# A gated attention and expert block: values in TensorE's waits, heads times values in two parts, and experts in turn by group with three places read early

## The reference, cut to what matters

```python
q = _qdq(x) @ _qdq(wq).T + bq
kv = cond @ wkv.T + bkv                      # k, v
attn = softmax(einsum('bnhd,bmhd->bhnm', q, k) * scale)
o = einsum('bhnm,bmhd->bnhd', attn, v)
x = x + tanh(g0) * (_qdq(o) @ _qdq(wp).T + bp)
...
scores = softmax(h @ gate_weight.T)          # 64 experts in 8 groups of 8
group_scores = scores.reshape(T, 8, 8).max(-1)
_, gidx = top_k(group_scores, 3)             # a token keeps 3 groups
topk_w, topk_i = top_k(where(smask, scores, 0), 6)
slot = flat * 96 + minimum(pos, 95)          # 96 places in each expert
out = (silu(buf @ Wg.T) * (buf @ Wu.T)) @ Wd.T
y = sum(out[slot] * topk_w)                  # six rows of each token
x = x + tanh(g1) * (y + shared(h))
```

## Time and profile before

| | |
|---|---|
| runs | 334.02, 332.68, 329.45 us; median 332.68 |
| profiled execution | 336.5 us, its span 334.6 us |
| granted TensorE clock, mean | 0.974 |
| busy share | PE 86%, DVE 52%, POOL 46%, ACT 33% |
| by stage (us from the span's start) | first loads and units 0 to 41; attention rounds 41 to 87; second norm, shared expert, routing and sort 87 to 131; experts 131 to 307; sums and stores 307 to 334.6 |

### The profile page before, as it was taken

The page is one execution under the profiler, slowest core; times in us unless marked ns, Lnnn a source line. Parts: engine busy times, 40 slices in busy tenths (PEclk is TensorE's granted clock), DMA queues, the critical chain, the costliest instruction groups (busy, mean ns, idle before and its releaser), DMA issues.

```text
span 334.6 us, 5615 instructions
## 1 busy us (share of the span) xinstructions
PE 289.3 (86%) x1963; PEld 178.2 (53%) x1964; DVE 173.8 (52%) x520; ACT 112.0 (33%) x276; POOL 153.8 (46%) x184
## 2 busy tenths in 40 slices
PE   0989858898898989688998799888988898999796
PEld 0455647666653556354554455545544454556674
DVE  2598538895897974342445333543433233333470
ACT  0593144667463343112222112211233233343101
POOL 8415101456605316725766566556655574335000
PEclk9999999999999999979999989999999999999769
DMA  6999940000495002337887788779877882116873
GB/s 220 362 352 379 408 167 2 3 5 2 167 357 192 0 2 63 110 112 257 284 297 245 261 275 297 276 243 317 261 266 249 308 284 100 49 48 198 317 317 125
DMA packets 28880, 68.40 MB, mean 204 GB/s; under 512 B 4374, under 2 KB 11702, under 8 KB 28214
## 3 DMA queue, kind: packets, MB, share of 16 engines
q1 hardware_dynamic: 21840, 54.41, 47.4%
q0 software_dynamic: 5376, 12.59, 10.9%
q10 hardware_dynamic: 1638, 1.05, 1.0%
HBM read 53.09 MB, written 14.94 MB: 203 GB/s over the span
## 4 chain that ended last, share of the span: by engine, by line
PE 71%; DVE 10%; issue 6%; another core or an unknown queue 5%; ACT 4%; DMA 3%; POOL 1%; SPq 0%; DVEq 0%; POOLq 0%
PE psum L1379 22%; PE psum L1396 7%; PE psum L1073 5%; PE psum L1399 5%; PE psum L1435 4%; PE psum L1370 4%; PE psum L1125 3%; PE psum L1268 3%; PE psum L1387 3%; DVE scratch L974 3%; PE psum L1138 2%; DVE order L973 2%; PE psum L1079 2%; PE psum L1440 2%
## 5 line engine op out<-in xcount | busy, mean ns | idle before, releaser
L1379 PE MATMUL psum<-stream,xn 128*96 128x352 f32 x256 | 90.1, 475 | 3.1 <-issue 2.1
L467 POOL DMA_INDIRECT parts<-ctxT,sidx x64 | 59.6, 932 | 62.0 <-ACT ctxT L646 48.4
L1009 DVE COPY rows<-psum 128x192 f32<-128x192 f32 x64 | 22.9, 357 | 86.5 <-PE psum L1388 39.6
L463 POOL DMA_INDIRECT scratch<-table,fetch x48 | 47.1, 982 | 19.7 <-issue 12.5
L1379 PEld LDWEIGHTS psum<-stream,xn 128*96 128x96 f32 x256 | 37.4, 164 | 33.1 <-issue 15.4
L639 ACT ACTIVATE rows<-psum 96x176 f32<-96x176 f32 x43 | 13.5, 314 | 67.4 <-PE psum L1379 36.6
L646 ACT ACTIVATE ctxT<-psum 96x256 f32<-96x256 f32 x64 | 20.8, 375 | 40.3 <-PE psum L1399 21.6
L1396 PE MATMUL psum<-stream,rows 128*96 128x256 f32 x128 | 33.8, 387 | 0.0
L1001 DVE COPY xn<-psum 128x256 f32<-128x256 f32 x48 | 20.1, 418 | 19.7 <-PE psum L1370 14.6
L1387 PE MATMUL psum<-ident,rows 96*128 96x96 f32 x64 | 16.7, 261 | 13.9 <-DVE rows L1009 9.0
L1387 PEld LDWEIGHTS psum<-ident,rows 96*128 96x128 f32 x64 | 9.2, 143 | 30.1 <-issue 24.9
(11 more groups left out here) (215 smaller groups left out, 464.7 us busy)
## 6 DMA issues: line engine op xcount, KB each, us to landing
stream<-wmain_in SPq DMA_DIRECT2D x64, 480.0 KB
parts<-zeros SPq DMA_DIRECT2D x1, 6144.0 KB, 28.4
stream<-parts SPq DMA_DIRECT2D x5, 1024.0 KB, 7.9
stream<-wrem_in SPq DMA_DIRECT2D x32, 112.0 KB
x<-x_in SPq DMA_DIRECT2D x2, 512.0 KB, 6.3
ctxT<-ctxT_in SPq DMA_DIRECT2D x2, 512.0 KB, 7.9
table<-rows SPq DMA_DIRECT2D x8, 128.0 KB, 8.8
parts<-ctxT,sidx POOLq DMA_INDIRECT x64
```

What stands on the lines that cost most here:

```text
L463: g.indirect_dma_start(gx[n % GBUF], None, table, bass.IndirectOffsetOnAxis(fetch[:, j, q:q + 1], 0)).then_inc(got_rows[n % GBUF], 16)
L467: g.indirect_dma_start(parts, bass.IndirectOffsetOnAxis(sidx[:, e:e + 1], 0), orow[e % OBUF], None).then_inc(out_done[e % OBUF], 16)
L1009: v.tensor_copy(hidT[e % 4], bank[6][:, 0:2 * CAP]).then_inc(hidT_done, 1)
L1379: last = t.matmul(bank[UP_BANK[e % (LAG + 1)]][0:CAP, 0:WG], gxT[:, k, CAP * (e % 4):CAP * (e % 4) + CAP], wgu[slot][:, k], start=(k == 0) ...
```

## The change

The program's order changes in four places, beside new banks.

1. Values are made tile by tile (`value_tile`). Tiles 0 and 1 come as before, tile 2 while TensorE waits for the transposed tokens, tiles 3 to 7 in rounds 0 to 2. Units, scores and the projection's weights move up.
2. `heads_times_values` is split from round 3 on: groups 1 and 2 of heads ahead of the scores, 3 and 0 behind the negated maxima. The last two tiles' products stand next to each other, the last in a bank of its own. VectorE's second part of the split maxima (`split_rest`) and the norm of tiles 0 to 3 come later.
3. Experts are worked in turn by group: first the first expert of each group, then the second, and so on; the weights are permuted on the host, and VectorE writes choice and weights in that order. Since a token keeps three groups, at least three of its six experts are worked before the last eight. Places 0, 1 and 2 are read after experts 53, 54 and 55.
4. TensorE sums tiles 0, 1, 4 and VectorE 2, 3, 5, 6, 7; three places are added ahead of the correction on TensorE, four on VectorE.

```diff
...
-PE_TILES, DVE_TILES = (0, 1, 4, 5), (2, 3, 6, 7)
-SUM_BANK = {0: 1, 1: 2, 4: 3, 5: 7}
-CORR_AT = {2: (4, 0), 3: (4, D), 6: (5, 0), 7: (5, D)}
-CORR_STEP = 2
+PE_TILES, DVE_TILES = (0, 1, 4), (2, 3, 5, 6, 7)
+SUM_BANK = {0: 1, 1: 2, 4: 3}
+CORR_AT = {2: (4, 0), 3: (4, D), 5: (5, 0), 6: (5, D), 7: (7, 0)}
+PE_STORES, DVE_STORES = ((0, 2), (4, 1)), ((2, 2), (5, 3))
+EARLY = TOPK - TOPG
+CORR_STEP = EARLY + 1
+
+
+def complete_at(k):
+    return EXPERTS - GROUPS - EARLY + k if k < EARLY else EXPERTS - TOPK + k
+
...
-V_BANK = (5, 4, 6, 7)
-UNIT_BANK = (0, 1, 2, 3, 0, 1, 5, 4)
+V_AT = ((5, 0), (5, D), (4, 0), (7, 0), (6, 0), (6, D), (7, 0), (6, 0))
+V_BEFORE = {0: 6, 1: 8}
+V_SHARED = {0: 2, 4: 6}
+WP_AT = (4, 256)
+UNIT_BANK = (0, 1, 2, 3, 0, 1, 5, 6)
 XQ_BANK = (6, 7, 6, 7)
 ST_BANK = 2
+PV_BANK = (6,) * 7 + (1,)
+PV_SPLIT = 3
 Y_BANK = (7, 7, 7, 7, 2, 3, 2, 3)
...
-        ranked = [cut(TILES * D).rearrange("p (b h) -> p b h", b=TILES) for _ in range(TOPK)]
+        place_rows = lambda: cut(TILES * D).rearrange("p (b h) -> p b h", b=TILES)
+        ranked = [place_rows() for _ in range(1, TOPK - 1)]
+        over = cut(TILES * EXPERTS).rearrange("p (b e) -> p b e", b=TILES)
+        ranked += [place_rows()]
+        cut(2 * (RING * MAINW + PAIRS * D) - TILES * (EXPERTS + (TOPK - 1) * D))
+        ranked = [place_rows()] + ranked
         overT = cut(TILES * P, EXPERTS).rearrange("p (b t) -> p b t", t=P)
-        over = cut(TILES * EXPERTS).rearrange("p (b e) -> p b e", b=TILES)
...
-            first_final = EXPERTS - TOPK
-            for e in range(first_final - OBUF + 1, first_final):
-                sp.wait_ge(out_done[e % OBUF], 16 * (e // OBUF + 1))
+            written = complete_at(0) - OBUF
             for k in range(TOPK):
-                e = first_final + k
-                sp.wait_ge(out_done[e % OBUF], 16 * (e // OBUF + 1))
+                while written < complete_at(k):
+                    written += 1
+                    sp.wait_ge(out_done[written % OBUF], 16 * (written // OBUF + 1))
                 if k < TOPK - 1:
                     sp.dma_start(ranked[k], rank_rows(k)).then_inc(got_ranked[k], 16)
...
             pool.wait_ge(xp_done, TILES)
             for b in range(2, TILES):
+                heads_to_int(b - 2)
                 if b == TILES - 1:
                     norm2_rstd(0)
-                heads_to_int(b - 2)
                 if 3 <= b < TILES - 1:
                     residual(b - 3)
             heads_to_int(TILES - 2)
...
                 if b >= 3:
                     project(b - 3)
             exponential(TILES - 1, 0)
+            exponential(TILES - 1, 1)
             heads_out(TILES - 2)
-            exponential(TILES - 1, 1)
             heads_row(TILES - 4)
+            heads_out(TILES - 1)
             act.wait_ge(nmr_done, 3)
             second_norm(0)
-            heads_out(TILES - 1)
             second_norm(1)
             heads_row(TILES - 3)
             second_norm(2)
...
...
-                v.tensor_scalar(sel[:, n], eout[:, n, 0:EXPERTS], CHOSEN, None, ALU.is_equal).then_inc(sel_done, 1)
+                v.tensor_scalar(in_turn(sel[:, n]), by_group(eout[:, n, 0:EXPERTS]), CHOSEN, None, ALU.is_equal).then_inc(sel_done, 1)
...
                     link(v.scalar_tensor_tensor(out=pexp, in0=eout[:, :, 0:EXPERTS], scalar=CHOSEN, in1=pexp, op0=ALU.is_equal, op1=ALU.mult))
+                    link(v.tensor_copy(in_turn(weight), by_group(pexp)))
                     dve.wait_ge(rankS_done, 1)
                 elif i % 2:
-                    link(v.scalar_tensor_tensor(out=one_rank, in0=rankS, scalar=float((i - 3) // 2), in1=pexp, op0=ALU.is_equal, op1=ALU.mult))
+                    link(v.scalar_tensor_tensor(out=one_rank, in0=rankS, scalar=float((i - 3) // 2), in1=weight, op0=ALU.is_equal, op1=ALU.mult))
...
             def attend(b):
+                if b >= 2:
+                    heads_normalised(b - 2, b % 2)
+                    if b + 1 < TILES:
+                        split_rest(b + 1)
+                    heads_scale(b - 2)
+                    heads_rscale(b - 2)
                 if b == TILES - 1:
                     stats2(b - 4)
                     norm2_veps(0)
-                if b >= 2:
-                    heads_normalised(b - 2, b % 2)
-                    heads_scale(b - 2)
-                    heads_rscale(b - 2)
+                if b == 2:
...
+                if b == 2:
+                    value_tile(7)
                 if b + 2 < TILES:
                     maximum(b + 2, 1)
                 if 4 <= b < TILES - 1:
                     stats2(b - 4)
                 if b + 2 < TILES:
                     maximum(b + 2, 0)
+                    if b == 1:
+                        value_tile(6)
                     split_max(b + 2)
-
...
+                    if b == 0:
+                        split_rest(b + 2)
+
+            maximum(0, 1)
+            maximum(0, 0)
+            split_max(0)
+            split_rest(0)
+            dve.wait_ge(wT_done, 2)
+            value_tile(2)
+            dve.wait_ge(tanh_done, 1)
+            v.tensor_scalar(bvp[:, 1], bvp[:, 1], tg[:, 0:1], None, ALU.mult).then_inc(tbp_done, 1)
+            maximum(1, 1)
             dve.wait_ge(w_psum, 3)
-            v.tensor_scalar(wscale[:], bank[5][:, 256:512], tg[:, 0:1], None, ALU.mult).then_inc(wT_done, 1)
-            for b in range(TILES):
+            v.tensor_scalar(wscale[:], bank[WP_AT[0]][:, WP_AT[1]:WP_AT[1] + 256], tg[:, 0:1], None, ALU.mult).then_inc(wT_done, 1)
+            maximum(1, 0)
+            split_max(1)
+            split_rest(1)
+            value_tile(3)
+            attend(0)
+            value_tile(4)
+            value_tile(5)
+            for b in range(1, TILES):
                 attend(b)
-            norm2_nmr(0)
             heads_normalised(TILES - 2, 0)
             heads_scale(TILES - 2)
             heads_rscale(TILES - 2)
+            norm2_nmr(0)
...
-            def heads_times_values(b):
+            def heads_times_values(b, groups=range(4)):
                 pe.wait_ge(exp_done, 2 * b + 2)
-                pe.wait_ge(headsT_done, b)
-                pe.wait_ge(v_done, b + 1)
-                if b >= 2:
-                    pe.wait_ge(oT_done, min(b - 1, TILES - 4))
-                for g in range(4):
+                pe.wait_ge(v_done, V_BEFORE.get(b, TILES))
+                if PV_BANK[b] == 6:
+                    pe.wait_ge(headsT_done, b)
+                    if b >= 2:
+                        pe.wait_ge(oT_done, min(b - 1, TILES - 4) - (0 not in groups))
+                else:
+                    pe.wait_ge(max_done, 2 * TILES)
+                for g in groups:
                     for i in range(4):
                         h = 4 * g + i
-                        last = t.matmul(bank[6][VW * i:VW * i + VW, TOK * g:TOK * g + TOK], vpad[:, b, h], probs[b % 2][:, TOK * h:TOK * h + TOK],
+                        last = t.matmul(bank[PV_BANK[b]][VW * i:VW * i + VW, TOK * g:TOK * g + TOK], vpad[:, b, h], probs[b % 2][:, TOK * h:TOK * h + TOK],
                                         start=True, stop=True)
-                last.then_inc(pv_psum, 1)
+                if 0 in groups:
+                    last.then_inc(pv_psum, 1)
...
...
                 scores_t(b)
                 if b >= 2:
                     heads_across(b - 2)
+                if b >= PV_SPLIT:
+                    heads_times_values(b - 1, (1, 2))
                 if b >= 3:
                     heads_row(b - 3)
+                if b == 0:
+                    value_tile(3)
+                elif b == 1:
+                    value_tile(5)
+                elif b == 2:
+                    pe.wait_ge(headsT_done, 1)
+                    value_tile(7)
                 if b + 2 < TILES:
                     scores(b + 2)
+                if b == 0:
+                    pe.wait_ge(v_done, 4)
                 negmax_across(b + 1)
-                if b >= 1:
+                if b == 0:
+                    value_tile(4)
+                if b >= PV_SPLIT:
+                    heads_times_values(b - 1, (3, 0))
+                elif b >= 1:
                     heads_times_values(b - 1)
+                if b == 1:
+                    pe.wait_ge(nm_done, 3)
+                    value_tile(6)
                 if b >= 3:
                     pe.wait_ge(nm_done, b + 2)
                     project(b - 3)
...
                 b = TILES - 1
                 scores_t(b)
-                heads_times_values(b - 1)
                 heads_across(b - 2)
                 heads_row(b - 3)
+                heads_times_values(b - 1)
+                heads_times_values(b)
                 pe.wait_ge(norm_done, b - 1)
                 heads_across(b - 1)
-                heads_times_values(b)
                 project(b - 3)
...
             scores(0)
-            xq_across(2)
-            xq_across(3)
             pe.wait_ge(xqT_done, 4)
             pe.wait_ge(v_done, 2)
```

(26 more changed lines are left out.)

84 lines of the change are left out of this document (46 added, 38 removed).

## The result

The change took **321.50 us** (median of 4 runs, 318.97 to 321.75) beside 333.13 for the kernel before (4 runs, 329.45 to 334.02): ratio 0.965 with a 95% interval of 0.957 to 0.974, 11.6 us faster. 319.6 was forecast. The profiled execution took 321.54 (span 319.7, before 334.6). A median here is that of all runs of a kernel, while ratios and their intervals leave out executions in a slower state (over 1.5% above the fastest of their kernel), so that a ratio need not be the quotient of two medians.

What follows compares the result with a forecast made beforehand. It took TensorE's serial work ahead of the loop and late place reads in the tail as bounds; -6.6 + 1.0 + 0 + 1.0 - 8.8 + 0.3 = -13.1 us, taking the median from 332.68 to 319.6 us, range 316 to 323.

Steps and rivals of the forecast that it cites:

- Ahead of the loop: Before the attention loop: moving six values tiles out of TensorE's series starts transposed scores at 34.2 instead of 40.80, -6.6 us.
- Values tiles in the loop: Attention rounds: tile 6 adds 0.65 and tile 7 adds 0.35, the other tiles fit into waits; +1.0 us.
- heads times values in two parts: Attention loop from round 3: half moves ahead of the scores, VectorE's maxima still set the round; 0 us.
- The end of attention: Behind the loop: later norm delays ScalarE's normalised rows, tile 7's product comes earlier; +1.0 us, bounds -0.5 and +2.5.
- rival 1: Tail: TensorE's clock falls all the same, tail gains only 5.3 us, time 323.1; chance 0.14.
- The reads: Expert stage: early reads of places 0 to 2 make no one wait; 0 us.
- The tail: After the experts: early reads and three TensorE tiles keep full clock, end at 325.8; -8.8 us, bounds -9.6 and -5.7.
- The rest: Among the experts: VectorE's copy of weights into the new order and the strided choice cost +0.3 us (0 to 0.8).
- 2 (given back in the loop): Attention: first window overruns in rounds 2 to 5, norm rows cost 2.5; 4.6 us more, 324.2; chance 0.13.
- 3 (reads late): Tail: first data come as late as now, only TensorE's smaller share helps; tail -2, 326.4; chance 0.10.
- 4 (stalls of "another core or an unknown queue"): Expert stage: an earlier start may move these 17 us of waits; doubled, 336.6; chance 0.05.
- range of 316 to 323: Whole kernel: the forecast's own range in us, from bounds of the tail and end of attention, each alone; chance 0.58.

Runs made afterwards that it cites:

- e10: e9 with heads times values in one piece (PV_SPLIT = 8 instead of 3): 322.85 us, ratio 0.967 to the kernel before.
- e5: The changed kernel run again, unaltered, beside other variants: 301.19 us, ratio 0.966 to the kernel before (311.77 there).
- e1: Only the change's attention part; expert order, reads and tile division as in the kernel before: 330.74 us, ratio 0.984 to the kernel before.
- e7: The changed kernel with all six places read after the 59th scatter and later, as before: 309.74 us, ratio 0.989 to the kernel before.
- e8: The changed kernel with tail tiles divided four on TensorE and four on VectorE, as before: 300.07 us, ratio 0.966 to the kernel before.
- e4: The changed kernel with four unused products in TensorE's two waits at the end of attention: 322.55 us, ratio 0.960 to the kernel before.
- e6: The changed kernel with both the norm placement of e3 and the fill products of e4: 298.63 us, ratio 0.958 to the kernel before.
- e9: The kernel of e6 run again in another comparison: 323.17 us, ratio 0.967 to the kernel before (335.57 there).
- e2: The kernel before with only the expert turn, early reads and three/five tile division: 329.16 us, ratio 0.985 to the kernel before.
- e11: The kernel before run once more, unaltered, for one profile beside e9, e10 and e12: 333.04 us.
- e3: The changed kernel with the norm of tiles 0 to 3 back in its old place on VectorE and GpSimd: 322.58 us, ratio 0.964 to the kernel before.
- e12: The kernel before with four unused products in TensorE's tail wait ahead of the overflow products: 335.76 us, ratio 1.001 to the kernel before.

## Why the prediction was right, and where not

- **Ahead of the loop, -6.6: right, -6.9.** The thread was VectorE's maxima and then TensorE, as worked out. The product took 0.49 us instead of 0.7 and unit 7 took 1.72 instead of 1.98, which I had named as the lower bound. (The terms as written add up to 34.3, not 34.2.)
- **Values tiles in the loop, +1.0, and heads times values in two parts, 0: together +1.1.** The round with tile 6 grew by 0.74 (0.65 forecast), the one with tile 7 by 0.19 (0.35), and the split costs 0.5 in all (e10) where I had 0; the sum came out because the last rounds in one piece are shorter than before by 0.04 to 0.13 each. VectorE's second part of the split maxima takes 0.21 to 0.22 us in every round (L805), as forecast, where its last three took 0.80 before.
- **The end of attention, +1.0: right at full clock, mis-sized where the clock falls.** The delay of the normalised rows is what I had: in e5, at full clock, from tile 7's transposed scores (71.7) to the shared product (84.7) are 13.0 us against 12.0 before, +1.0. What I left out is that the longer wait leaves TensorE half idle, and that its clock may fall behind it. In the profile after it fell: +1.8 more up to the shared product and +1.2 in the shared products behind it; the choice is made 3.0 us later (101.5 in the profile after, 98.5 in e5). I had rival 1 at the wrong end of the kernel: I looked for the fall where it had been, not where the change makes a new wait. Of five profiles with this wait (after, e1, e5, e7, e8) the fall came in two, after and e7; in four with the wait filled (e4, e6, e9, e10) in none. That is too few to show that filling prevents it. The change's median, 1.9 us above the forecast, probably has this fall in it: three of its four runs had a mean clock of 0.975 to 0.977, the fourth had 0.993 and took 318.97. But only one of them was profiled, and there the clock fell a second time, at the start of the experts, behind a stretch with TensorE busy 1.40 of 4 us:

```profile
140.00:144.00 4.00, 3.18 (x12) 2.05 (x12) 1.98 (x8) 0.31 (x1) 0.37 (x1) 0.54 0.19 56
144.00:148.00 4.00, 4.00 (x13) 1.93 (x10) 0.85 (x4) 0.96 (x3) 1.84 (x2) 0.60 0.53 181
```

Between 136 and 152 us it fell in ten of the fourteen profiles, before and after alike; only e5 to e8 kept it. Which of the two falls a run with 0.993 was spared, no run shows.
- **The reads, 0 on their own: right.** The expert stage is 150.5 us with the early reads (e5) and without (e7).
- **The tail, -8.8: right to the tenth for the profile it was made against, and too large for the median.** That profile's tail had a long fall of the clock and the execution took 3.8 us more than the median from which I then took the whole gain. Against the old tail at full clock (23.2 and 24.6) the new one, 18.2 to 19.4 in eight profiles, gains 4 to 6, and by its runs e2 gains about 5. That the tenth came out is luck, and so in part is the total: with 5 for 8.8 the sum is -9.3; the medians are 11.6 apart, with an interval of 9 to 14. The steps held: no gap on TensorE, overflow at full clock, both engines ending together (VectorE at 316.06, TensorE at 315.44), with ScalarE's copy of TensorE's last tile the last link where I had VectorE. What carries it is the early reads (e7); with them TensorE has no wait in the tail, and its clock did not fall there.
- **The rest, +0.3: not seen.** The expert stage differs by more between two executions of one kernel.
- **Rivals.** 1 (clock in the tail): 1.00 in 303 to 314, TensorE busy 11.00 of 11 us, and in the eight other profiles with early reads it fell nowhere between the identity products and TensorE's last product. The Trainium skill (TensorE: Matmul & The Clock Gate, Part 4) says that transposes don't count as busy in the way that products do; ahead of the rank products it changed nothing. At the end of attention it may bear: of TensorE's 2.06 us of work in 76 to 80 about 1.3 are transposes, and with four products more there the clock held in four profiles. But e1, e5 and e8 kept 1.00 with the same transposes, so no run here shows that it decides. 2 (given back in the loop): 1.1 of it, and the clock at the end of attention was the part not named. 3 (reads late): e7 is what it would have been, and worse than I priced it (-2 for the tail; 28.9 against 27.4 measured, +1.5), for I had not counted that three places now stand ahead of the overflow. 4 (stalls of "another core or an unknown queue"): 7% of the chain after, 5% before, none in e5 to e8 and 3 to 8% in all the other profiles; the change doesn't move them. The range of 316 to 323 held, but the bounds that it is said to come from, each alone, give 318.1 to 322.7; no row stands behind the 316.

The profiled spans differ by 14.9 us, not 13.1: -6.9 and +1.1 up to the end of the loop, +1.0 and, by the clock, +3.0 at the end of attention, -4.3 of the expert stage, -8.8 of the tail. The clock and the expert stage offset each other there. The medians are 11.6 apart. That they don't have the stage's 4.3 us is likely after e11, not shown.

## What to carry to other kernels

Data that can be read before the last writer is done (here, since the experts' order completes half of each token's places eight experts ahead) shortens a serial tail more than a better division of the work in it: with four tiles on either engine the tail is 20.4 us (e8) where before it was 23.2 to 27.4, and the division took another 1.4. Take such a gain from more than one profile of before: one with a long tail makes it look larger than the runs have it (8.8 us against 5). Where a change makes a new wait for TensorE, price the wait and, separately, a fall of its clock behind it; filling the wait with products that nobody reads costs tenths (0.4 us from e5 to e4, 1.0 from e3 to e9), and the runs agreed within 1 us in e6 and e9, not in e4 (3.3 us). But fill only where TensorE sets the end: where data do, the full clock only waits sooner (e12).

## What was not expected of the hardware

- The same instruction stream with the same busy time (2.06 of 4 us) kept the clock at 1.00 in e5 and lost it in the profile after; in e7, 0.64 in 80 to 84 us and 0.50 behind it. In e12 it also fell in the loop, from 1.00 in 40 to 44 us to 0.70 and 0.50 behind stretches with TensorE busy 2.38 and 2.78 of 4 us, which the change fills; e12's first shared product is 3.4 us later, and its transposed scores of tiles 0 to 7 are 40.5 us apart instead of 36.7. No run isolates that.
- The expert stage is 145.0 us long from the first to the last up product in e5 and 165.5 in the profile after, by the same instructions. Busy time in a stretch of it, of the profile after and then of e5:

```profile
190.00:220.00 30.00, 27.78 (x136) 15.73 (x134) 12.56 (x35) 6.49 (x21) 18.97 (x20) 1.00 0.85 291
```

```profile
190.00:220.00 30.00, 30.00 (x151) 17.59 (x149) 14.51 (x42) 7.97 (x25) 23.18 (x23) 1.00 0.96 320
```

In the first, ScalarE and VectorE wait up to 3.7 us (4.7 elsewhere in the stage) for something that the trace calls "remote", and TensorE does 136 instructions where it does 151 in the second. What it is stays open: 20 us of 320 that no edit of this study touched.
